# Graph transformer layer, edge walks: destinations broadcast three batches at a time into two buffers

## The reference, cut to what matters

```python
def _gat_conv(x, edge_index, W, att_src, att_dst, bias, heads, out_ch, concat):
    h = (x @ W).reshape(n, heads, out_ch)
    a_src = jnp.sum(h * att_src[None], axis=-1)
    a_dst = jnp.sum(h * att_dst[None], axis=-1)
    e = jax.nn.leaky_relu(a_src[src] + a_dst[dst], NEG_SLOPE)
    m = jax.lax.stop_gradient(jax.ops.segment_max(e, dst, num_segments=n))
    p = jnp.exp(e - m[dst])
    denom = jax.ops.segment_sum(p, dst, num_segments=n)
    alpha = p / denom[dst]
    out = jax.ops.segment_sum(h[src] * alpha[..., None], dst, num_segments=n)
```

## Time and profile before

| what | us |
|---|---|
| median of three runs | 3769.68 |
| lowest and highest run | 3755.59, 3773.42 |
| the profiled execution | 3798.44 |
| its span, first to last instruction | 3796.7 |

### The profile page before, as it was taken

The page is one execution under the profiler, slowest core; times in us unless marked ns, Lnnn a source line. Parts: engine busy times, 40 slices in busy tenths (PEclk is TensorE's granted clock), DMA queues, the critical chain, the costliest instruction groups (busy, mean ns, idle before and its releaser), DMA issues. The chain is left out here.

```text
span 3796.7 us, 66505 instructions
## 1 busy us (share of the span) xinstructions
PE 2719.0 (72%) x14765; PEld 2077.4 (55%) x14766; DVE 2286.5 (60%) x6866; ACT 1182.9 (31%) x4644; POOL 1816.9 (48%) x1892
## 2 busy tenths in 40 slices
PE   8577767677766776785666666666666666699998
PEld 6455555555555555574555544455444444557666
DVE  6766766666766766784555544445655565635445
ACT  5533333333333333332122111122222321343342
POOL 0355555555555555502555555666555554501111
PEclk9788998888888888897788878777777777599999
DMA  5566666666666666513444464544333333321220
GB/s 190 150 180 174 182 185 180 173 180 182 181 174 181 182 181 178 165 37 95 122 136 137 123 180 116 153 127 106 100 97 100 101 103 97 134 86 52 78 86 12
DMA packets 272861, 512.09 MB, mean 135 GB/s; under 512 B 53920, under 2 KB 176779, under 8 KB 272658
## 3 DMA queue, kind: packets, MB, share of 16 engines
q0 software_dynamic: 118128, 361.70, 34.2%
q1 hardware_dynamic: 140006, 134.66, 12.8%
q10 hardware_dynamic: 14524, 13.40, 1.0%
HBM read 463.94 MB, written 49.57 MB: 135 GB/s over the span
## 5 line engine op out<-in xcount | busy, mean ns | idle before, releaser
L921 PE MATMUL PS<-w_G,w_S 128*128 128x260 f32 x3520 | 982.0, 435 | 356.5 <-DVE ACC L1011 228.7
L1318 POOL DMA_INDIRECT weights<-table,w_idx x880 | 845.0, 960 | 727.3 <-issue 293.7
L808 POOL DMA_INDIRECT w_G<-table,w_idx x880 | 847.1, 963 | 677.4 <-issue 286.0
L921 PEld LDWEIGHTS PS<-w_G,w_S 128*128 128x128 f32 x3520 | 726.1, 215 | 531.3 <-issue 258.6
L1505 PE MATMUL PS<-weights 128*128 128x257 f32 x1760 | 648.4, 513 | 353.0 <-DVE ACC L1697 215.7
L1505 PEld LDWEIGHTS PS<-weights 128*128 128x128 f32 x1760 | 407.3, 253 | 480.6 <-issue 286.0
L999 DVE TENSOR_TENSOR w_G<-w_G,PS 128x512 f32<-128x512 f32 x660 | 432.4, 683 | 64.5 <-ACT PS L831 33.9
L844 ACT ACTIVATE w_G<-w_G 128x64 f32<-128x64 f32 x1760 | 443.9, 335 | 0.2
L1011 DVE TENSOR_TENSOR ACC<-ACC,PS 128x520 f32 x464 | 321.2, 692 | 183.9 <-PE PS L921 90.6
L1340 ACT ACTIVATE w_PW<-w_Z 128x4 f32<-128x4 f32 x220 | 45.3, 206 | 1091.8 <-DVE w_Z L1682 841.6
L1697 DVE TENSOR_TENSOR ACC<-ACC,PS 128x257 f32 x464 | 196.3, 423 | 279.5 <-issue 181.5
(11 more groups left out here) (322 smaller groups left out, 3321.2 us busy)
## 6 DMA issues: line engine op xcount, KB each, us to landing
w_DR<-rows SPq DMA_DIRECT2D x220, 128.0 KB
weights<-rows SPq DMA_DIRECT2D x220, 128.0 KB
weights<-in_L_ffn_w SPq DMA_DIRECT2D x16, 1024.0 KB, 7.7
w_G<-table,w_idx POOLq DMA_INDIRECT x880
weights<-table,w_idx POOLq DMA_INDIRECT x880
table<-ACC SPq DMA_DIRECT2D x49, 260.0 KB
xbuf<-XR SPq DMA_DIRECT2D x8, 1040.0 KB
XR<-xbuf SPq DMA_DIRECT2D x7, 1040.0 KB, 5.3
```

The costliest lines, as they stand in the source:

```text
L808: pool.indirect_dma_start(G[:, r, b, :], None, table, IndexOn(ap=idx[:, r, b:b + 1], axis=0)).then_inc(fetched[r], 16)
L921: last = pe.matmul(PS[:, 2 * j + a, 0:W // layer.banks], lhsT, rhs, start=b == slots[0], stop=b == slots[-1])
L1318: pool.indirect_dma_start(G[:, r, b, :], None, table, IndexOn(ap=idx[:, r, b:b + 1], axis=0)).then_inc(fetched[r], 16)
```

## The change

In both walks DR has two buffers of CHUNK = 3 batches in place of three buffers of one. A transfer brings 1536 destinations, 3 KB to each partition, 384 KB in all; a walk has 74 of them, the last with one batch. Transfers 0 and 1 go without a wait; transfer c waits until 3(c-1) comparisons are done, which frees its buffer. The comparison reads its third of the buffer and waits for the semaphore of the buffer, `row_in[u]`. In `walk2` SyncE's program issues a chunk at every third n, and the other transfers keep their places in it. The room comes from other tiles: in `walk` `diag` lies on two places of S; in `walk2` DR becomes a tile of its own, ST and q move into the arena, and YC and YT lie on HS, which is finished by then.

```diff
 walk:
-    AHEAD = 3
+    CHUNK = 3
-        DR = sb(tag + "DR", [P, AHEAD, B * P], BF16)
+        DR = sb(tag + "DR", [P, 2, CHUNK, B * P], BF16)
-        wide_path = sb("x" + tag + "wide_path", [P, P + H * P])
-        off = wide_path[:, 0:P]
-        diag = wide_path[:, P:].rearrange("p (h q) -> p h q", h=H)
+        off = sb("x" + tag + "off", [P, P])
+        diag = S[:, 4:6, :, :].rearrange("p r b q -> p (r b) q")
-            for n in range(NB):
-                if n >= AHEAD:
-                    sp.wait_ge(st_ready, n - AHEAD + 1)
-                sp.dma_start(DR[:, n % AHEAD, :], rows16[n * B:(n + 1) * B, :].rearrange("b e -> (b e)").partition_broadcast(P)).then_inc(row_in[n % AHEAD], 16)
+            for c in range(-(-NB // CHUNK)):
+                if c > 1:
+                    sp.wait_ge(st_ready, (c - 1) * CHUNK)
+                w = min(CHUNK, NB - c * CHUNK)
+                sp.dma_start(DR[:, c % 2, 0:w, :].rearrange("p n e -> p (n e)"),
+                             rows16[c * CHUNK * B:(c * CHUNK + w) * B, :].rearrange("b e -> (b e)").partition_broadcast(P)).then_inc(row_in[c % 2], 16)
             def turned_hot(b_):
-                dve.wait_ge(row_in[b_.slot(AHEAD)], b_.round(AHEAD) * 16 + 16)
+                u, v = divmod(b_.slot(2 * CHUNK), CHUNK)
+                dve.wait_ge(row_in[u], b_.round(2 * CHUNK) * 16 + 16)
 ...
 walk2, besides the same:
-        DR = place("w1_DR", [P, AHEAD, B * P // 2]).bitcast(BF16)
+        DR = sb("w1_DR", [P, 2, CHUNK, B * P], BF16)
-        ST = sb("w1_ST", [P, 2, B, P], BF16)
+        ST = place("w1_ST", [P, 2, B, P // 2]).bitcast(BF16)
+        q = place("w1_q", [P, 2, QK])
-        YC = sb("YC", [P, D])
-        YT = sb("YTC", [P, 2, P])
+        after_mine = HS[:, :, :].rearrange("p u c -> p (u c)")
+        YC = after_mine[:, 0:D]
+        YT = after_mine[:, D:2 * D].rearrange("p (k q) -> p k q", k=2)
             for n in range(NB):
-                row(n)
+                if n % CHUNK == 0:
+                    chunk(n // CHUNK)
```

More of the change, by code:

```diff
@@ L741, in walk @@
         hot = sem(tag + "hot")
-        row_in, st_ready = [sem(f"{tag}row_in{r}") for r in range(AHEAD)], sem(tag + "st_ready")
+        row_in, st_ready = [sem(f"{tag}row_in{u}") for u in range(2)], sem(tag + "st_ready")
         spread = sem(tag + "spread")
@@ L961, in turned_hot @@
             def turned_hot(b_):
-                dve.wait_ge(row_in[b_.slot(AHEAD)], b_.round(AHEAD) * 16 + 16)
+                u, v = divmod(b_.slot(2 * CHUNK), CHUNK)
+                dve.wait_ge(row_in[u], b_.round(2 * CHUNK) * 16 + 16)
                 if not b_.fixed or b_.base > 1:
                     dve.wait_ge(spread, b_.n - 1)
-                dve.tensor_scalar(ST[:, b_.slot(2), :, :].rearrange("p b e -> p (b e)"), DR[:, b_.slot(AHEAD), :], lanes[:, 0:1], None, ALU.is_equal).then_inc(st_ready, 1)
+                dve.tensor_scalar(ST[:, b_.slot(2), :, :].rearrange("p b e -> p (b e)"), DR[:, u, v, :], lanes[:, 0:1], None, ALU.is_equal).then_inc(st_ready, 1)
             def logits(n, r, q, between=lambda b: None):
@@ L1169, in walk2 @@
         fetched = [sem(f"w1_fetched{r}") for r in range(RING)]
-        row_in = [sem(f"w1_row_in{r}") for r in range(AHEAD)]
+        row_in = [sem(f"w1_row_in{u}") for u in range(2)]
         staged, st_ready, spread, z_ready, weighed, scaled, summed, merged, own, split, parts_ready, released = (
@@ L1204, in walk2 @@
         gp, nkm, ks = early("gp", [P, 2]), early("nkm", [P, 1]), early("ks", [P, 1])
-        YC = sb("YC", [P, D])
-        YT = sb("YTC", [P, 2, P])
+        after_mine = HS[:, :, :].rearrange("p u c -> p (u c)")
+        YC = after_mine[:, 0:D]
+        YT = after_mine[:, D:2 * D].rearrange("p (k q) -> p k q", k=2)
         WQ = sb("WQ", [P, 2, QK])
-        q = sb("q", [P, 2, QK])
         QT = sb("QT", [P, P])
@@ L1285, in raw_rows, with chunk @@
                     sp.dma_start(XR[0:LAST, TILES - 1, 0:D], x[(TILES - 1) * P:N, :]).then_inc(xc_in[6], 16)
[L1287 to L1290, removed]
+            def chunk(c):
+                if c > 1:
+                    sp.wait_ge(st_ready, (c - 1) * CHUNK)
+                w = min(CHUNK, NB - c * CHUNK)
+                sp.dma_start(DR[:, c % 2, 0:w, :].rearrange("p n e -> p (n e)"),
+                             rows16[c * CHUNK * B:(c * CHUNK + w) * B, :].rearrange("b e -> (b e)").partition_broadcast(P)).then_inc(row_in[c % 2], 16)
             for n in range(NB):
-                row(n)
+                if n % CHUNK == 0:
+                    chunk(n // CHUNK)
                 if n == 2:
```

## The result

The changed kernel takes 3753.26 us (median of 20 runs, 3746.90 to 3766.84), the kernel before in the same comparison 3767.14 us (20 runs, 3755.59 to 3777.01). The ratio is 0.9962, with a 95% interval of 0.9953 to 0.9972: 14 us faster, 11 to 18.

What follows compares the result with a forecast made beforehand. Two edge walks, loops of four unsaturated engines limited by hand-overs, were taken to bound the kernel. Terms 0 + 0 + 0 + 0.5 + 0 + 0 gave +0.5 us, forecast 3770 us, with 8 in 10 from 3731 to 3797 us.

Steps and rivals of the forecast that it cites:

- Step 1: Both walks, fewer, larger transfers: SyncE saves 146 issues of 320 ns per walk, 93 us, worth 0 since it waits.
- Step 2: Comparisons' wait for destination rows: four steps give 27.9 us, 384 KB land in 3.9 to 11.8 us; worth 0.
- Steps 5 and 6: SyncE's other transfers in walk 2, tightest at the clears, under 5 us left; new places in memory: 0 each.
- Step 4: Starts of the walks: more rows ahead of the first gathers; 0 in walk 1, 0.5 us in walk 2.
- step 3: DMA bytes and engines' time in the walks: same bytes, saving between nothing and two thirds, taken as 0 for time.
- The fall of the gathers from 120 to 57 packets: Walk 1, 765.5 to 767.5 us, while a row transfer passed: cited for row transfers holding up gathers.
- The forecast's own sign of being wrong: Either walk: the prediction is wrong if a walk changes its length by over 10 us.
- The faster rival: Walks: row transfers hold up the gathers; 39 to 58 us saved, 3731 us, at best 3712 us; chance 0.18.
- sign of recognition: Logits in the walks: "remote" waits fall by some 40 us and the DMA share falls if row transfers delayed gathers.
- the rows' 12.4% of the DMA time: Walks: rows' part of DMA time beside gathers, applied to 465.7 us of "remote" waits, giving 58 us.
- The slower rival: Walks: one 384 KB burst starves a gather, 1.07 us at 49 bursts, 53 us, 3823 us; chance 0.11.
- The 177 us of transfer time: Row transfers: the skill's timings, by straight line, save 177 us over 146 chunks; counts only where a transfer is waited for.

Runs made afterwards that it cites:

- e6: Whole change, but each 384 KB transfer cut into 384 pieces of 1 KB by 32-byte gaps: 1.0002 of the kernel before, which took 3103.18 us.
- e9: Kernel before with six one-batch buffers in the change's memory, 128 KB sent behind every comparison, six batches ahead: 0.9996 against 3765.99 us.
- e15: Kernel before with six one-batch buffers in the change's memory, a transfer after every comparison, six batches ahead: 0.9993 against 3769.24 us.
- e13: The whole change run again against the kernel before: 3750.69 us, 0.9955 against 3769.24 us.
- e12: Kernel before without row broadcasts after the first three batches of each walk (edges' weights not right): 0.9976 against 3805.44 us.
- e16: Kernel before without row broadcasts after the first three batches of each walk (edges' weights not right): 0.9969 against 3769.24 us.
- set 5: Whole change, three-transfer bursts, six one-batch buffers, and no later rows, each against the kernel before at 3769.24 us: 0.9955, 0.9977, 0.9993, 0.9969.
- e14: Whole change, but each chunk brought by three 128 KB transfers in a burst: 0.9977 of the kernel before, which took 3769.24 us.
- set 4: Three-transfer bursts, 384 KB in 1 KB pieces, and no later rows, each against the kernel before at 3805.44 us: 0.9978, 0.9983, 0.9976.
- e10: Whole change, but each chunk brought by three 128 KB transfers in a burst: 0.9978 of the kernel before, which took 3805.44 us.
- e11: Whole change, but each 384 KB transfer cut into 384 pieces of 1 KB by 32-byte gaps: 0.9983 of the kernel before, at 3805.44 us.

## Why the prediction was off by 14 us

**What held.** Step 1: 146 of 148 issues bring 384 KB, and SyncE's saved issues are worth nothing, since it still waits 1121.0 and 813.6 us. Step 2: 384 KB land in 5.1 us (e6, at the quicker pace), between the 3.9 and 11.8 us of the forecast and near the lower end, as it took; nothing waits, and the lead alone gives 0.9996 and 0.9993. Steps 5 and 6: no wait for DR around the clears, and comparisons at 346 and 352 ns; e9 and e15 have the new places too and no loss. Step 4: the first comparison comes at 139.7 us for 138.8, and nothing is late behind it; 0.9 us instead of 0, and 0.3 us in e13 (139.1).

**What failed** is step 3, "I take 0 for the time, because the walks' DMA share is 0.51 to 0.64 and nobody waits for q1". Its premise is right, its conclusion isn't. The rows cost 9 to 12 us in e12 and e16 with nobody waiting for them, and the change gives back 14 to 17 us (0.9962, 0.9955). I took the list of those who wait for a transfer as the list of those it delays, and put at 0 both what larger transfers save and what their new moments do. The zero is a property of the pace: at 3104 us, where GpSimd's issue sets the batch, it is right (0.9999); at 3767 us it is off by 14 us, 0.03 us for each of 440 batches.

I also misread. The fall of the gathers from 120 to 57 packets doesn't need the row beside them: GpSimd, waiting for TensorE, had issued nothing from 763.88 to 766.03 us, so there was less to move.

```profile
762.93 0.95 POOL L808 DMA_INDIRECT w_G<-table,w_idx  x1 [0.30 <-issue]
766.03 0.95 POOL L808 DMA_INDIRECT w_G<-table,w_idx  x1 [2.15 <-PE PS L921]
```

And the two queues together fill 44% of the sixteen engines in those two microseconds (24.3 and 20.1%). So "that gathers slow beside q1" is not shown there, nor by the mean cost of a gather's packet from 700 to 1200 us, which does not fall when the rows go: 187 ns before, 189 in e15, 192 in e13 and 194 in e16.

The forecast's own sign of being wrong, a walk that changes by over 10 us, is met by the two main profiles (21.6 and 24.8 us), which are no measure of the change; e13 and e15 differ by 5.5 and 4.4 us.

**The faster rival** ("row transfers were holding up the gathers") had the sign, and a chance of 0.18. Its size was 39 to 58 us and its sign of recognition a fall of the "remote" waits by some 40 us. From profile to profile they move either way. In set 5 they are 526.3 us (e15), 510.8 (e14), 502.5 (e13) and, with no rows at all, 495.7 us (e16), a fall of 31 us; in set 4 they are 470.2 us in e10 and 517.2 us without rows (e12). The lines of e16:

```profile
DVE w_Z L1671 <- remote: 259.2, 66, 11.7
DVE w_Z L977 <- remote: 236.5, 56, 5.7
```

So the rows are not what these waits are made of, since some 500 us of them are there without rows, and taking the rows' 12.4% of the DMA time as 12.4% of the waits was a sum over the wrong pool. What the rows cost in all is the 9 to 12 us that the runs without them give. That bound could not come from the trace of before; it took the kernel without the rows.

**The slower rival** (one long burst "starves a gather", +53 us) is refuted here twice: three transfers in one burst are no slower than one behind each comparison (e14 0.9977, e15 0.9993), and the one large transfer is at least as good. The Trainium skill, page "DMA: Bandwidth & Descriptors", section "Bandwidth", with its rule that DMAs want batching towards 1 MiB, had the sign right: fewer engine-us for the same bytes, here 6.5 to 7.1 a batch for 8.5. The 177 us of transfer time that I worked out from its figures never were on the path as a whole; 14 us came off it.

**What stays open.** How a row transfer costs time. That the rows lengthen the pauses would fit, and the profiles don't bear it out: counted as above, walk 1 has 45 pauses with 98.5 us in e15, 41 with 88.5 us in e13, and 48 with 107.0 us in e16, which has no rows. Nor is the traffic on the DMA engines told apart from SyncE's issues and the signals, which the change and the runs without rows take away with it. Whether it is the larger pieces or the fewer transfers that give the second part: e10 and e11 stand side by side at 0.9978 and 0.9983, which speaks for the pieces (one transfer in small pieces is no better than three), but the whole change was not in that set. How the 14 us split between the walks. And what sets the pace.

## What to carry to other kernels

An empty list of waits for a transfer says that the transfer is early enough; it doesn't say that it is free. Where it shares the DMA engines with something that is waited for, the bound for its price is a run without it, made at the pace at which the difference was seen. Before a difference of a few tenths of a per cent is explained by two profiles, their times have to be held against the medians: here one stood 31.3 us over its median and the other 6.1 us under, 37 of the 51 us between them.

## What the runs showed of the hardware

The same kernel ran at three paces, each steady within a set: 3103 to 3105 us in three sets (a spread of 8 us over the 33 runs of the first), 3766 to 3769 us on record and in two sets, 3805 us in one. Only the two loops with gathers differ, 5.0 to 5.1 and 6.5 to 6.7 us a batch, and with them the granted clock (means 0.91 to 0.92 and 0.83 to 0.84). A change that was worth nothing at one pace, 0.9992 and 1.0003, was worth 0.45% at the other, 0.9955. So a verdict of this size holds for the pace at which it was taken.

The rows' engine time for 128 KB from 700 to 1200 us, at the two slower paces: 8.3 to 8.5 us in one transfer behind each comparison (e9, e15, before), 7.2 and 7.7 us in bursts of three (e10, e14), 7.0 us in one transfer of 384 KB cut into 1 KB (e11), 6.5 and 7.1 us in one cut into 3 KB (e13 and the profile after). So most of the saving is there without larger pieces. e11's line, for 24 transfers or 72 batches:

```profile
q1 hardware_dynamic: 9600, 9.44, 6.3%
```

384 KB landed in 5.1 us (e6), where a single 128 KB had landed within 3.9 us at the slower pace.
